# Setup of a two-layer graph kernel reordered, and edge types brought by broadcast transfers

## The chip, the cores and the metric

One core of one Trainium2 chip runs the whole program. The metric is the device time of one execution in microseconds (us); the median of several executions is compared.

## The reference, cut to what is computed

The graph has 1,250 nodes with 512 features and 40,000 edges, sorted by destination. There are 32 relation types, each a mix of 8 bases of 512x512.

```python
h = maximum(layernorm(x), 0)
weight = einsum('rb,bio->rio', w_comp, bases)          # 32 x 512 x 512
h_rel  = einsum('ni,rio->rno', h, weight)
x = x + segment_sum(h_rel[etype, src] * edge_weight, dst) + h_bias
h = maximum(layernorm(x), 0)
g = h @ W.T + b                                        # degree-normalised convolution with self loops
x = x + relu(segment_sum(norm * g[row], col))
```

## The kernel before, in words

**Main loop.** Nodes are cut into 20 destination tiles of 64, and the edges into 335 slots of 128 edges; a slot belongs to one tile. POOL (GpSimd) issues one indirect DMA per slot (L693), which gathers 128 rows of 2,304 bytes from the table `tab0_d` (normalised features as a float16 high and low half, and a one-hot part) into a ring of `UN` = 8 buffers `gath`. PE (TensorE) runs 12 matmuls (L1493, source features against a selection matrix `sel`) and one (L1499, counts for layer 1) for each slot. DVE (VectorE) makes `sel` and `oh_ad` for a batch of up to four slots (`select`, L1125 to L1131), in a ring of three batches, from three columns per slot: `dloc` (place in the tile), `code` (side and block of the source) and `val` (8 numbers, the row of `w_comp` for the edge's type times its weight).

**Steps tied to slots.** `STEPS[s]` lists what each engine does after slot s, in the same order on every engine; `PROD[s]` lists the products with the bases (L1513) that PE weaves into slot s + 1. A `flush` (after slots 12, 24, 37, 48, ...) empties the PSUM banks of a tile, ACT (ScalarE) the high half, DVE the low one. `bsplit` splits one base of 1 MB in two halves, ACT L811 and then DVE L1245; `wt` turns and splits W1 (L1540, L816, L1250). `largest` and `scale` find the powers of two by which bases and W1 are scaled: ACT first takes the sum of squares of each of the 8 bases and of W1 (`squares_of`, L767), and PE waits for all nine at slot 7 before it transposes them (L1360). `turn` (L1522) and `proj` (L1533) are the two steps of layer 1's projection.

**Values.** A value group is eight slots. `types(k)` on PE copies the types of eight slots to all 128 partitions with two matmuls (L1388) of a `band` matrix against `typ16`; DVE compares them with each partition's relation number (`one_hot_types`, L1070) and makes the next `band` (L991); `look(k)` on PE multiplies the one-hot with `wparts` (L1395); DVE reduces and scales (L1079, L1082), ACT takes the high half (L753) and DVE the low half (L1089). Three groups (`VEARLY`) are done in the setup, the others from `STEPS`.

**One shared bank.** The steps types, look, turn, proj, wt, largest and scale all use PSUM bank `MB`. The list `SHARED` is their order, and in `shared_free` PE waits for the reader of the step before: after `types(k)` that is DVE's `one_hot_types(k)`.

**Setup.** SP (SyncE) loads edges and x, writes x to `xbase_d` from SBUF (L567), and loads base 0, then bases 1 to 4 once the edge records are gathered into `padr` (`s_padr`). ACT normalises x tile by tile (L745, L741); the low halves of tiles 0 to 6 are made by POOL (L672), those of tiles 7 to 9 by DVE (`low`, L974) behind most of its setup. SP writes each finished tile to the table (L577), then issues bases 5 to 7, the two bias rows, W1 and the first x rows. DVE turns `padr` into columns (L960 to L969), checks that the edges are in order (the `flag`), makes scales, and then `code` and `dloc` for all 336 columns. A run-time branch on `flag` follows (work for edges in any order; not taken with these inputs). DVE and ACT do the three value groups ahead of it.

Of the kernel before, what the change touches and what calls it, by code (L numbers as in the profile page):

```python
# [6 lines left out]
def gnn_kernel(nc, x, src, dst, etype, ew, bases, w_comp, h_bias, W1, b1, out):  # L7
# [5 lines left out]
    P = 128  # L13
# [20 lines left out]
    TN = 64  # L34
# [49 lines left out]
    VEARLY = 3  # L84
    SLV = NVAL * VB
# [4 lines left out]
    x1_d = nc.dram_tensor("x_layer1", [N, D], f32, kind="Internal").ap()  # L90
    cext_d = nc.dram_tensor("counts_any_order", [2, P, NT * N], f16, kind="Internal").ap()

    ctx = ExitStack()
    with ctx:
# [34 lines left out]
        typ16 = sb("typ16", [P, C0, P], bf16)  # L129
# [9 lines left out]
        rel = sb("rel", [P, 1], f32)  # L139
        ident = sb("ident", [P, P], f32)  # L140
# [47 lines left out]
        w_in = u_t[:, 0:FT, :]  # L188
        TZ = 5
# [7 lines left out]
        blk_c = take_z(i32, P)  # L197
# [15 lines left out]
        e_wt = carve(h_t[:, :])(f32, EC)[0:EP, :]  # L213
# [16 lines left out]
        row_f, same, pack_f = rec_w[0:1, 0:SLP], rec_w[0:1, SLP:3 * SLP], rec_w[0:1, 3 * SLP:3 * SLP + SLP // WPACK]  # L230
# [24 lines left out]
        LOWS, BEARLY = 7, 5  # L255
# [3 lines left out]
        SQ_SETUP, SC_AT, BS_AT, WT_AT = BEARLY, 7, 10, 38  # L259
# [102 lines left out]
        SHARED = []  # L362
        for v in range(VEARLY):
            SHARED += [("types", v), ("look", v)]
        for ss in STEPS:
            SHARED += [k for k in ss if k[0] in ("types", "look", "turn", "proj", "wt", "largest", "scale")]
# [11 lines left out]
        s_win = sem("s_win")  # L378
        s_bias = sem("s_bias")
# [25 lines left out]
        s_scaled = sem("s_scaled")  # L405
# [143 lines left out]
        def _(sp):  # L549
# [20 lines left out]
            for n in range(1, BEARLY):  # L570
                load_base(n)
# [1072 lines left out]
```

## Time and profile before

| | |
|---|---|
| median of 3 runs | 642.95 us (640.42 to 645.22) |
| the profiled execution | 640.33 us, of which the span from first to last instruction is 638.4 us |
| mean granted TensorE clock | 0.912 |
| PE busy | 503.5 us |
| DVE busy | 351.0 us |
| POOL busy | 352.3 us |
| DMA | 129.97 MB, mean 204 GB/s |

The profile is of one execution. Busy time of PE is that of pipelined matmuls, whose ends are modelled. The share of the span tells little by itself, since the setup (to about 65 us), the slots (to about 560 us) and the tail have different limits.

### The profile page before, as it was taken

Reading aid. Unit: us, or ns where it says so; the run is one execution under the profiler, and the core shown is the slowest. Engines: PE = TensorE matmul, PEld = TensorE weight load, DVE = VectorE, ACT = ScalarE, POOL = GpSimd, SP = SyncE. Lnnn points to the kernel's source line nnn. Section 1 sums busy time; section 2 is a strip of 40 time slices with the busy share of each in tenths; the row PEclk is TensorE's granted clock in tenths of the full one; section 3 lists DMA queues with packets and bytes.
Section 4 is the critical chain, followed back from the end, with each engine's and each line's share of the span. In section 5 each row is a group of like instructions: output and inputs, shape, how many; then the busy total and the mean of one; then the engine's idle time right before and its main releaser. Section 6 shows DMA issues by size and latency. Waiting matters only on the chain.

```text
span 638.4 us, 15882 instructions
## 1 busy us (share of the span) xinstructions
PE 503.5 (79%) x5908; PEld 321.6 (50%) x5908; DVE 351.0 (55%) x974; ACT 151.8 (24%) x272; POOL 352.3 (55%) x473
## 2 busy tenths in 40 slices
PE   3031455878978989999999998999987876889997
PEld 1020345545654656665656655565655554545443
DVE  7798178775763445765755655646644321364121
ACT  3492244432220011121220312202201000251021
POOL 3423648765772776675757757767577777400000
PEclk9565767799997999999999999999999978699999
DMA  9888945565783886785866858868768877514042
GB/s 291 300 335 298 346 124 162 143 197 157 219 257 88 231 265 198 211 255 168 265 190 191 264 155 244 255 180 258 230 202 263 237 235 239 160 27 139 2 97 67
DMA packets 44932, 129.97 MB, mean 204 GB/s; under 512 B 9053, under 2 KB 9678, under 8 KB 44854
## 3 DMA queue, kind: packets, MB, share of 16 engines
q0 software_dynamic: 27040, 99.60, 52.5%
q1 hardware_dynamic: 16860, 28.13, 13.5%
q8 instruction: 58, 0.95, 0.6%
q10 hardware_dynamic: 954, 1.13, 0.6%
q14 instruction: 20, 0.16, 0.1%
HBM read 117.83 MB, written 11.00 MB: 202 GB/s over the span
## 4 chain that ended last, share of the span: by engine, by line
PE 50%; DMA 18%; DVE 15%; issue 6%; ACT 5%; POOL 3%; ACTq 1%; SPq 1%; POOLq 0%; DVEq 0%
PE PS L1513 21%; PE PS L1493 16%; DMA gath<-rows_layer,srcs 13%; PE PS L1589 7%; PE PS L1533 5%; DMA u_t<-in_L_gnn_W_dram 4%; DVE zt L1209 2%; POOL gath L693 2%; DVE room_b L1209 2%; ACT room_b L811 2%; DMA edge_records<-room_c 1%; DVE room_b L1245 1%; DMA w1t<-edge_records,w1t 1%; PE PS L1499 1%; ACT zt L800 1%
## 5 line engine op out<-in xcount | busy, mean ns | idle before, releaser
L693 POOL DMA_INDIRECT gath<-rows_layer,srcs x335 | 335.9, 1003 | 179.1 <-PE PS L1499 95.9
L1493 PE MATMUL PS<-sel,gath 128*128 128x48 f16 (+7 forms) x4020 | 299.7, 207 | 58.6 <-DMA gath<-rows_layer,srcs 28.3
L1493 PEld LDWEIGHTS PS<-sel,gath 128*128 128x128 f16 x4020 | 235.2, 103 | 169.4 <-issue 93.5
L1513 PE MATMUL PS<-room_b,zt 128*128 128x512 f16 x480 | 168.3, 392 | 1.6 <-DVE sel L1131 1.5
L1513 PE MATMUL PS<-room_b 128*128 128x512 f16 (+1 forms) x480 | 150.4, 381 | 0.3 <-DVE room_b L1209 0.2
L1499 PE MATMUL PS<-oh_ad,gath 128*128 128x30 bf16 (+7 forms) x335 | 65.0, 194 | 0.0
L753 ACT CAST val<-val_f 128x64 f16<-128x64 f32 x42 | 11.1, 264 | 215.2 <-DVE val_f L1082 215.2
L1125 DVE TENSOR_TENSOR masks<-iota_n,dloc 128x24 bf16<-128x24 f32 (+12 forms) x92 | 17.8, 193 | 78.9 <-issue 40.5
L1513 PEld LDWEIGHTS PS<-room_b 128*128 128x128 f16 (+1 forms) x480 | 47.4, 104 | 14.3 <-issue 1.0
L1513 PEld LDWEIGHTS PS<-room_b,zt 128*128 128x128 f16 x480 | 45.4, 100 | 8.9 <-issue 2.7
L1131 DVE TENSOR_TENSOR sel<-masks,val 128x192 f32<-128x192 bf16 (+12 forms) x92 | 38.6, 419 | 0.0
L1589 PE MATMUL PS<-zt,room_c 128*128 128x512 f16 (+1 forms) x160 | 36.2, 379 | 0.0
L1499 PEld LDWEIGHTS PS<-oh_ad,gath 128*128 128x128 bf16 x335 | 34.4, 103 | 3.1 <-issue 2.6
L1533 PE MATMUL PS<-w1t,hT_t 128*128 128x512 f16 (+1 forms) x120 | 30.1, 405 | 7.4 <-DVE oh_t L1070 5.9
L1079 DVE TENSOR_REDUCE val_f<-PS 128x64 f32<-128x192 f32 x42 | 14.9, 356 | 35.3 <-PE PS L1395 31.3
L1209 DVE SCALAR_TENSOR_TENSOR room_b<-PS,room_b 128x512 f16<-128x512 f32 x40 | 24.8, 682 | 12.9 <-ACT room_b L800 12.9
L1070 DVE TENSOR_SCALAR oh_t<-PS,rel 128x256 bf16<-128x256 f32 x42 | 20.2, 480 | 19.2 <-PE PS L1388 17.5
L800 ACT ACTIVATE room_b<-PS 128x512 f16<-128x512 f32 x40 | 20.6, 601 | 40.1 <-PE PS L1499 37.7
L1127 DVE TENSOR_TENSOR oh_ad<-iota_n,code 128x120 bf16<-128x120 f32 (+12 forms) x92 | 29.6, 322 | 0.0
L1209 DVE SCALAR_TENSOR_TENSOR zt<-PS,zt 128x512 f16<-128x512 f32 x40 | 24.8, 682 | 8.6 <-ACT zt L800 8.6
L803 ACT CAST room_c<-c_i 128x320 f16<-128x320 int32 (+1 forms) x40 | 16.1, 450 | 46.3 <-DVE c_i L1215 46.3
L1589 PEld LDWEIGHTS PS<-zt,room_c 128*128 128x128 f16 (+1 forms) x160 | 16.0, 100 | 18.2
(208 smaller groups left out, 446.0 us busy)
## 6 DMA issues: line engine op xcount, KB each, us to landing
room_b<-in_L_gnn_bases_dram SPq DMA_DIRECT2D x8, 1024.0 KB, 8.2
gath<-rows_layer,srcs POOLq DMA_INDIRECT x335
x_t<-x_base SPq DMA_DIRECT2D x19, 128.0 KB, 5.0
u_t<-in_x_dram SPq DMA_DIRECT2D x9, 256.0 KB, 6.4
x_base<-u_t SPq DMA_DIRECT2D x9, 256.0 KB
x_layer<-x_t SPq DMA_DIRECT2D x18, 128.0 KB
u_t<-x_layer SPq DMA_DIRECT2D x18, 128.0 KB, 2.6
out_dram<-u_t SPq DMA_DIRECT2D x18, 128.0 KB
```

Source lines behind the costliest of these rows:

```text
L693: pool.indirect_dma_start(out=gath[:, s % UN, :], out_offset=None, in_=tab0_d[:, :], in_offset=bass.IndirectOffsetOnAxis(ap=srcs[:, s:s + ...
L800: a.activation(zt[q % 2][:, 0, f, :, TN * h:TN * (h + 1)], zbank(f), ACT.Copy, scale=ZDOWN).then_inc(s_hi, 1)
L1070: v.tensor_scalar(oh_t[:, k % 2, :, :].rearrange("p j e -> p (j e)"), PS[:, MB, 0:VB // 4 * P], rel[:, :], None, ALU.is_equal).then_inc(s_ ...
L1125: v.tensor_tensor(mask, iota_n[:, 0:w].unsqueeze(1).to_broadcast([P, k, w]), dloc[:, s:s + k].unsqueeze(2).to_broadcast([P, k, w]), ALU.is ...
L1127: v.tensor_tensor(oh_ad[:, there, 0:k, 0:HA * w], iota_n[:, 0:HA * w].unsqueeze(1).to_broadcast([P, k, HA * w]), code[:, s:s + k].unsqueez ...
L1131: v.tensor_tensor(sel[:, there, 0:k, 0:NB * w].rearrange("p k (b d) -> p k b d", b=NB), mask.unsqueeze(2).to_broadcast([P, k, NB, w]), val ...
L1209: v.scalar_tensor_tensor(lo, zbank(f), ZDOWN, hi, ALU.mult, ALU.subtract).then_inc(s_lo, 1)
L1493: mm(there, gath[:, s % UN, D * t + P * f:D * t + P * (f + 1)], sel_parts[:, here, k, 0:NB * w, u], start=first and t == 0 and u == 1, sto ...
L1499: mm(there, oh_r[:, s % UN, :], oh_ad[:, here, k, 0:HA * w], start=first, stop=True, skip_group_check=True).then_inc(s_used, 1)
L1513: last = mm(PS[0:r, PBANK[q], :], zt[q % 2][:, t, f, b, 0:r], base_hl[:, b, u, f, :], start=(m == 0), stop=(m == NM - 1))
L1533: last = mm(PS[0:r, MB, :], hT_t[:, s, f, 0:r], w1t[:, t, f, :], start=(f == s == t == 0), stop=(f == FT - 1 and s == 1))
L1589: return mm(PS[0:r, FBANK[j], :], there, u_part(i, t)[0:ROWS[i], :], start=first, stop=True, skip_group_check=not first)
```

## The change

- **W1 first.** W1 is loaded behind x into the unused part of `room_b` (`w_early`), and ACT squares it in the setup. A second load (`s_win2`) brings it to `w_in` for `wt`, which moves from slots 38 to 41 to slots 54 to 57.
- **x_base.** The ten writes from SBUF become one transfer from x in DRAM to `xbase_d`, behind the last base.
- **Loads.** Bases 0 to 3 follow `s_padr`; bases 4 to 7 follow the table and the types of groups 1 and 2. Bias rows wait for all codes.
- **Low halves.** All ten are DVE's, put between its setup steps; POOL makes none.
- **Types.** Two matmuls and `band` per group go. `typ16` is written to DRAM (`types_d`), and for each group SP issues four transfers, each of which copies two slots' types (512 bytes) to 32 partitions, in a ring of three (`TRING`). `one_hot_types` reads SBUF. Steps of kind types leave `SHARED`. Slots within a group are held in another order, which changes access patterns only.
- **Branch and values.** The branch comes ahead of the values. Then one group and 24 columns of codes are done before the first slot; groups 1 to 3 come with slots 0 to 8 and the other 312 columns of codes at slot 4.
- `largest` moves from slot 7 to 9; `bsplit` from slots 10, 13, ..., 31 to 13, 15, 17, 19, 26, 28, 30, 33.

```diff
+        BEARLY = 4
...
+        SQ_SETUP, SC_AT, WT_AT = BEARLY, 9, 54
+        BS_AT = [13, 15, 17, 19, 26, 28, 30, 33]
+        SQ_AT = {4: 0, 5: 1, 6: 3, 7: 6}
+        CFIRST, CODES_AT = VEARLY * VB, 4
...
-        for v in range(VEARLY, NVAL):
-            STEPS[VB * v - 23].append(("types", v))
-            STEPS[VB * v - 18].append(("look", v))
+        for v in range(1, NVAL):
+            at = max(VB * v - 23, 3 * (v - 1))
+            STEPS[at].append(("types", v))
+            STEPS[max(VB * v - 18, at + 2)].append(("look", v))
...
+            sp.dma_start(w_early, W1.rearrange("(c p) i -> p c i", p=P)).then_inc(s_win, 16)
...
+            sp.wait_ge(s_padr, 16 * C0)
+            for n in range(BEARLY):
+                load_base(n)
+            def load_types(v):
+                if v >= TRING:
+                    sp.wait_ge(s_oht, v - TRING + 1)
+                for t in range(FOUR):
+                    s = VB * v + SPG * t
+                    sp.dma_start(types[R * t:R * (t + 1), v % TRING, :],
+                                 types_d[s:s + SPG, :].rearrange("(p j) e -> p (j e)", p=1).to_broadcast([R, SPG * P])).then_inc(
+                                     s_types[v % TRING], 16)
+            sp.wait_ge(s_loc, 2 * C0)
+            for c in range(C0):
+                sp.dma_start(types_d[P * c:P * (c + 1), :], typ16[:, c, :]).then_inc(s_typd, 16)
             for i in range(NT):
-                sp.wait_ge(s_xin[i], 16)
-                sp.dma_start(xbase_d[P * i:P * i + XROWS[i], :], x_in[0:XROWS[i], i, :]).then_inc(s_xbase, 16)
...
+                if i == 4:
+                    sp.wait_ge(s_typd, 16 * C0)
+                    load_types(0)
+                sp.wait_ge(s_h0lo, i + 1)
                 sp.dma_start(tab0_d[P * i:P * i + XROWS[i], 0:2 * D],
                              table_of(i).rearrange("p s d -> p (s d)")).then_inc(s_tab0, 16)
+            for v in range(1, TRING):
+                load_types(v)
             for n in range(BEARLY, NB):
                 load_base(n)
+            sp.dma_start(xbase_d[:, :], x[:, :]).then_inc(s_xbase, 16)
             sp.wait_ge(s_flag, 1)
...
             sp.wait_ge(s_tab0, 16 * (NT + 3))
-            sp.dma_start(w_in, W1.rearrange("(c p) i -> p c i", p=P)).then_inc(s_win, 16)
-            sp.wait_ge(s_xbase, 16 * NT)
+            sp.dma_start(w_in, W1.rearrange("(c p) i -> p c i", p=P)).then_inc(s_win2, 16)
+            load_types(TRING)
+            sp.wait_ge(s_cols, 2)
...
+            sp.wait_ge(s_xbase, 16)
             load_x(0)
             load_x(1)
...
+            for s in range(VEND):
+                for kind, k in STEPS[s]:
+                    if kind == "types" and k + TRING < NVAL:
+                        load_types(k + TRING)
+                    elif kind == "x1" and k < NT - 1:
+                        keep_x1(k)
...
-            for i in range(LOWS):
-                pool.wait_ge(s_h0hi, i + 1)
-                t = table_of(i)
-                g.tensor_tensor(t[:, 1, :], x_in[0:XROWS[i], i, :], t[:, 0, :], ALU.subtract).then_inc(s_h0lo_pool, 1)
...
             def one_hot_types(k):
-                dve.wait_ge(s_types, k + 1)
+                dve.wait_ge(s_types[k % TRING], 16 * FOUR * (k // TRING + 1))
                 if k >= 2:
                     dve.wait_ge(s_look, k - 1)
-                v.tensor_scalar(oh_t[:, k % 2, :, :].rearrange("p j e -> p (j e)"), PS[:, MB, 0:VB // 4 * P], rel[:, :], None,
+                v.tensor_scalar(oh_t[:, k % 2, :, :].rearrange("p j e -> p (j e)"), types[:, k % TRING, :], rel[:, :], None,
                                 ALU.is_equal).then_inc(s_oht, 1)
...
-            def types(k):
-                shared_free(pe, ("types", k))
-                pe.wait_ge(s_band, k + 1)
-                for j in range(VB // 4):
-                    last = mm(PS[:, MB, P * j:P * (j + 1)], band[:, j, :], typ16[:, VB * k // P, :], start=True, stop=True)
-                last.then_inc(s_types, 1)
             def look(k):
                 shared_free(pe, ("look", k))
+                pe.wait_ge(s_oht, k + 1)
...
                     elif kind == "largest":
                         shared_free(pe, ("largest", 0))
-                        pe.wait_ge(s_sqb, NB + 1)
+                        pe.wait_ge(s_sqb, NB)
```

## Rows read from the trace of the kernel before

**Rows 1.** Windows: us, busy us (count) of PE, PEld, DVE, ACT, POOL, granted clock, DMA share, GB/s

```profile
200.00:300.00 100.00, 93.95 (x1218) 61.02 (x1217) 55.43 (x158) 17.30 (x39) 68.34 (x70) 1.00 0.72 213
62.00:64.00 2.00, 0.00 (x0) 0.00 (x0) 2.00 (x9) 1.91 (x3) 1.06 (x1) 0.50 1.04 391
78.00:80.00 2.00, 0.00 (x0) 0.00 (x0) 0.00 (x0) 1.17 (x1) 0.00 (x0) 0.50 1.05 333
```

**Rows 2.** Timeline, PE, setup to slot 25: start, us, instruction, idle before and releaser

```profile
65.74 0.98 PE L1493 MATMUL PS<-sel,gath 128*128 128x80 f16 x12 [7.45 <-DVE sel L1131]
73.91 0.68 PE L1493 MATMUL PS<-sel,gath 128*128 128x80 f16 x12 [0.61 <-DMA gath<-rows_layer,srcs]
80.98 0.37 PE L1360 MATMUL PS<-ident,sq 128*12 128x128 f32 x1 [6.37 <-ACT val L767]
91.98 0.82 PE L1493 MATMUL PS<-sel,gath 128*128 128x88 f16 x6 [5.36 <-DVE zt L1209]
113.86 0.78 PE L1493 MATMUL PS<-sel,gath 128*128 128x80 f16 x6 [6.24 <-DVE zt L1209]
```

**Rows 3.** Timeline, setup, DVE and POOL beside each other

```profile
4.41 0.28 DVE L895 TENSOR_SCALAR ident<-w1t,column 128x128 f32<-128x128 f32 x1
27.71 6.04 POOL L672 TENSOR_TENSOR zt<-u_t,zt 128x512 f16<-128x512 f32 x5 [5.12 <-ACT zt L741]
28.99 1.12 DVE L962 TENSOR_SCALAR w1t<-w1t 128x3 f32<-128x3 f32 x1
32.58 3.76 DVE L967 TENSOR_SCALAR w1t<-w1t 128x128 f32<-128x128 f32 x3
36.25 0.63 DVE L969 CAST typ<-w1t 128x128 bf16<-128x128 f32 x3
49.02 1.87 DVE L974 TENSOR_TENSOR room_c<-u_t,room_c 128x512 f16<-128x512 f32 x3
50.99 0.15 DVE L1043 TENSOR_SCALAR stats<-bound 128x1 int32<-128x1 int32 x1
```

**Rows 4.** Timeline, first and later gathers of POOL

```profile
55.37 1.15 POOL L693 DMA_INDIRECT gath<-rows_layer,srcs  x1 [19.16 <-issue]
65.61 0.95 POOL L693 DMA_INDIRECT gath<-rows_layer,srcs  x1 [0.30 <-issue]
```

**Rows 5.** Timeline, issues of SP

```profile
51.29 1.59 SPq L558 DMA_DIRECT2D room_b<-in_L_gnn_bases_dram  x3
52.92 0.77 SPq L581 DMA_DIRECT2D hb_t<-in_L_gnn_h_bias_dram  x1
55.74 0.39 SPq L607 DMA_DIRECT2D u_t<-in_L_gnn_W_dram  x1
```

**Rows 6.** DMA issues: target, source, queue, count, KB each, us to landing

```profile
hb_t<-in_L_gnn_h_bias_dram SPq DMA_DIRECT2D x1, 256.0 KB, 14.1
u_t<-in_L_gnn_W_dram SPq DMA_DIRECT2D x1, 1024.0 KB, 23.1
zt<-in_L_gnn_w_comp_dram ACTq DMA_DIRECT2D x4, 1.0 KB, 5.1
```

**Rows 7.** Timeline, PE, types of a group and what follows

```profile
300.27 0.27 PE L1388 MATMUL PS<-typ,band 128*128 128x128 bf16 x2
300.38 0.20 PE L1493 MATMUL PS<-sel,gath 128*128 128x72 f16 x1
```

**Rows 8.** Waits of PE, 115 to 200 us: us in total, times, longest

```profile
PE PS L1533 <- DVE oh_t L1070: 4.5, 1, 4.5
```

**Rows 9.** Waits of PE, whole span

```profile
PE PS L1493 <- DMA gath<-rows_layer,srcs: 28.3, 36, 2.2
PE PS L1533 <- DVE oh_t L1070: 5.9, 3, 4.5
```

**Rows 10.** Chain that ended last: start, us, what

```profile
193.00 5.30 PE PS L1533 x12
241.43 2.76 PE PS L1533 x12
```

More of the change, by code:

```diff
@@ L84, in gnn_kernel @@
     VEARLY = 3
+    FOUR = P // R
+    SPG = VB // FOUR
+    TRING = 3
     SLV = NVAL * VB
@@ L361, in gnn_kernel @@
         VEND = max(s for s, ss in enumerate(STEPS) if ss or PROD[s]) + 1
-        SHARED = []
-        for v in range(VEARLY):
-            SHARED += [("types", v), ("look", v)]
+        SHARED = [("look", 0)]
         for ss in STEPS:
-            SHARED += [k for k in ss if k[0] in ("types", "look", "turn", "proj", "wt", "largest", "scale")]
+            SHARED += [k for k in ss if k[0] in ("look", "turn", "proj", "wt", "largest", "scale")]
         SHARED += [("turn", NT - 1), ("proj", NT - 1)]
@@ L493, in shared_free @@
             kind, k = SHARED[n - 1] if n else ("first", 0)
-            if kind == "types":
-                eng.wait_ge(s_oht, k + 1)
-            elif kind == "look":
+            if kind == "look":
                 eng.wait_ge(s_vsum, k + 1)
@@ L1018, in _ @@
-            dve.wait_ge(s_slotmm, 1)
-            begins = PS[0:1, CB, 0:SLP].rearrange("p (g k) -> p g k", k=WPACK)
-            link(v.tensor_copy(pack_f, begins[:, :, WPACK - 1]))
-            for k in reversed(range(WPACK - 1)):
-                there = pack_f if k else slots[0:1, :]
-                link(v.scalar_tensor_tensor(there, pack_f, float(1 << WBITS), begins[:, :, k], ALU.mult, ALU.add))
+            low(0)
+            low(1)
+            columns_max(0)
+            dve.wait_ge(s_slotmm, 1)
@@ L1038, in _ @@
             v.reduce_sum(bad, same[:, 0:NSAME + SL + 1], AX.X).then_inc(s_have, 1)
+            for i in range(8, NT):
+                low(i)
             def powers(lo, hi):
@@ L1447, in _, with look @@
                 pe.wait_ge(s_any_zero, FT + 1)
+            def look(k):
+                shared_free(pe, ("look", k))
+                pe.wait_ge(s_oht, k + 1)
+                for j in range(VB // 4):
+                    last = mm(PS[:, MB, 12 * NB * j:12 * NB * (j + 1)], oh_t[:, k % 2, j, :],
+                              wparts[:, :, :].rearrange("p s c -> p (s c)"), start=True, stop=True)
+                last.then_inc(s_look, 1)
+            pe.wait_ge(s_wparts, 1)
+            look(0)
             window = {}
@@ L1549, in _ @@
                 for kind, k in STEPS[s]:
-                    if kind == "types":
-                        types(k)
-                    elif kind == "look":
+                    if kind == "look":
                         look(k)
```

249 lines of the change are left out of this document (117 added, 132 removed).

## The prediction, made before the changed kernel was run

> **What bounds the kernel now.** Read the windows first: from 200 to 300 us PE is busy 93.95 of 100 us at granted clock 1.00 [rows 1], so once the slots run, what counts is PE's own work and its few waits. The setup is different. In the timeline of PE [rows 2] the first slot starts at 65.74 us; slot 7 starts at 73.91; then PE waits 6.37 us for the squares of W1 and goes on at 80.98; slot 13 starts at 91.98, after 5.36 us of waiting for DVE's flush; slot 25 at 113.86, after 6.24 us for the same. Every microsecond won there by slot 25 stays won unless a gather gives it back, since from there PE is nearly always busy. The DMA windows tell why W1 was late: at 62 to 64 us the engines move 391 GB/s at a share above 1, at 78 to 80 us still 333 [rows 1]. Transfers of one queue land in their order: the bias row issued at 52.92 [rows 5] took 14.1 us [rows 6] and landed at 67.0, W1 issued at 55.74 took 23.1 and landed at 78.8. This order decides most of what follows.
>
> **Part 1: low halves go from POOL to DVE.** While POOL makes low halves (from 27.71 us, seven of them), a DVE instruction on 3 columns takes 1.12 us and three on 128x128 take 3.76 us, 1.25 each; alone, the same kinds take 0.15 us (on one column) and 0.28 us [rows 3]. The stretch L960 to L969, which ends at 36.9 us, holds three such long small instructions (L962, L964 and L965, about 1.1 us each) and the three of 1.25, so it should shrink by about 3 x 0.95 + 3 x 0.97 = 5.7 us. DVE pays ten low halves of 0.62 us (1.87 / 3 [rows 3]), seven more than before, 4.4 us. It gets back 4.8 us, summed from the starts of the instructions between 36.9 and 41.9 us in the same timeline: `band` and its rows 1.0, the packing of windows 1.1, and the check of the order of edges and `wparts` (0.95 and 1.75, moved into waits before `padr`). I let `padr` be ready 1.7 us sooner, as the ten x_base writes no longer stand beside the record writes (0 to 3 us, my estimate). Sum: the last low half ends at 50.9 - 5.7 - 1.7 + 4.4 - 4.8 = 43 us (50.9 is the end of the last low half [rows 3]).
>
> **Part 2: the table.** SP now stands at tile 4 until `typ16` has been written to DRAM. These writes are queued behind bases 0 to 3 (4.2 MB issued at about 26 us; at 0.35 MB per us they end at 38 to 39 us), so I take 40 us for that wait, 42 for the four issues of group 0, and 45.5 for the last table issue. The first gather, at 55.37 before [rows 4], comes at about 49. The first `sel` also moves: flag at 43 us, scales and packing 3 us, the 13 small code instructions of 24 columns about 2.3 us, one value group 1.5 us, one batch 0.9: about 51 us. With the landing of a gather, the first slot starts at about 54 us in place of 65.74, so 11 us sooner (8 to 13).
>
> **Part 3: the queue behind the table.** This is what eats the gain. Behind the last table, SP issues eight type transfers (at about 0.5 us each, 4 us; an issue of a base took 1.59 / 3 = 0.53 [rows 5]), then bases 4 to 7 (4.2 MB), x_base (2.56 MB), W1 again (1.05 MB) and only then the types of group 3. Before, 3.1 MB, two bias rows and W1 stood there. DVE needs group 3 at slot 6, and PE's `look(3)` at slot 8 needs that one-hot: PE can't pass slot 8, and DVE's later work is queued behind the same wait. By then 17 gathers of 0.295 MB (128 x 2,304 bytes) have been issued, 5.0 MB. At 0.37 MB per us, between the 0.391 and 0.333 of [rows 1], the 8.1 + 5.0 = 13.1 MB that begin at about 50 us end at 85 us. So the wait for W1 at slot 7 (80.98 us) is gone, and one for types at slot 8 takes its place. Gathers alone don't bring slot 8 there: under this load one took from 65.61 [rows 4] to 73.91 [rows 2], 8.3 us, and they came some 1.4 us apart, which makes slot 8 possible at 54 + 8 x 1.5 = 66. What ends last without the types would be base 7 and its square: (4.3 + 4.7) / 0.37 = 24.5 us, 74.5, and 2 us on ACT, 76.5. Group 4's types are queued behind the bias rows and the x rows (1.05 MB more, 3 to 4 us), and DVE meets them at step 9 ahead of the scales. From there: one-hot and look 86, slots 9 and 10 88, group 4 at 88.7, scales 2.3 us, 91, and flush(0), now with no `bsplit` ahead of it, lets slot 13 start at 92. **That is 0 against 91.98** [rows 2] (9 us sooner if the types aren't what ends last, 4 later if the copy is slow).
>
> The type transfers after slot 16 I cost at nothing: a group is loaded some 24 slots, over 30 us, ahead, and the nearest rows, four transfers of 1.0 KB in the setup, landed in 5.1 us [rows 6]. If a wait ahead of them on SP (for x1 rows) ate the lead, a group would cost up to 5.1 us, once or twice.
>
> **Part 4: flush(1).** Before, `bsplit` 3 and 4 at slots 19 and 22 stood ahead of the flush at 24, and PE waited 6.24 us [rows 2]. Now four splits end by 19 and the next comes at 26. A flush alone costs PE about 2 us. Gain 4.2 us (2 to 5). The other four splits are as many as fit before slot 37 in both versions: 0 (-1 to +2).
>
> **Part 5: types off PE and out of the shared bank.** In steady running two types matmuls delay the next slot by 300.38 - 300.27 = 0.11 us [rows 7]; groups 5 to 41 make 37 x 0.11 = 4.1 us. The waits are worth more. `proj` waited for `one_hot_types` 4.5 us once, at 188 to 193 us [rows 8], because the step types(12) stood between flush(5) and proj(0); it is now free to run beside the flush. After that idle time the 12 matmuls took 5.30 us, where the next projection took 2.76 [rows 10]: nearly twice, as at a granted clock of 0.50 (1.2 GHz) against 1.00 (2.4 GHz). So this place is worth 4.5 + 2.5 = 7 us. The other waits of this kind are 5.9 - 4.5 = 1.4 [rows 8, 9] and about 2 in smaller lines of the same view (L1522 and L1388), 3.4 together. From 200 us on (3.3 of matmuls, 3.4 of waits) I count half, 3.4, since PE also waits 28.3 us for gathers [rows 9], and time won ahead of a gather that isn't there is lost again. With 0.8 of matmuls ahead of 200 us and the 7: 11.2 us (6 to 15). Moving `wt` to slots 54 to 57 moves its waits of 0.6 to 2 us each to a place with less of DVE's work beside them; of those I count 1.5 us as gone (-1 to 4). DVE's `band` (0.41 us a group) and the cheaper one-hot are off the path: 0.
>
> **Sum.** 0 + 4.2 + 11.2 + 1.5 = 17 us less than 640.33, the profiled execution (638.4 of span and 1.9 around it), so 623. That execution is 2.6 us under the median, 642.95, so the forecast is 626 us, 2.6% less.
>
> **Rivals.** *A: the types of group 3 are not late* (the queue doesn't keep its order, or the copy is quick). Then base 7's squares end last at 76.5: another 9 us, 617. For it: nothing else in the table of steps needs more before slot 9. Against: the two landings of [rows 5, 6], in order of issue. *B, slower: the copy from DRAM to DRAM holds the queue.* No row shows such a copy. At the 391 GB/s of [rows 1] its 2.56 MB take 6.6 us; it decides the sign from the point where it takes 17 us more, 24 us, 0.11 MB per us, so that group 3 lands after 102 us. All that a slower copy adds shows one for one at slot 8, up to 650 if it takes 30 us. A milder form: with 10 of 16 engines it takes 10.5 us, 4 more, 630. No row here shows which; by the rule the forecast would be 630. *C: the gains after slot 25 go back to the gathers.* Then of part 5 only the place at 193 us and a little more stay: 5 to 7 us less, 632. *D: the setup is won, but nothing of it lasts*, because DVE's code columns (13 instructions on 312 columns, some 6 us) and groups 1 to 3, now among slots 0 to 8, become the limit. DVE has them done inside the wait for group 3, so that is no addition to the forecast, but it caps rival A at about 5 us.
>
> **Chances.** Forecast 0.42 (618 to 634), A 0.18 (610 to 618), the milder B 0.12 and C 0.12 (628 to 637), no net change 0.08, B in full 0.08. Range 611 to 640. Differences under 1% (6.4 us) can hardly be told from no change. Faster by over 1%: 0.80; within: 0.12; slower: 0.08.
>
> **What the profile after would show.** L967 near 0.3 us each and no L672; the last table issue at 45 us; the first gather at 49, the first slot at 54; a wait of PE of 15 us or more at `look(3)` released by DVE's one-hot, and DVE idle before it for a DMA of `types`, to 85 us; W1's second load landing just before; slot 13 at 92, slot 25 at 109; no wait of L1533 for the one-hot. I am wrong if the wait at slot 8 ends before 77 or after 95 us, if DVE waits for types after slot 16, or if waits for gathers grow by as much as the types' matmuls and waits shrink.

## The result, and the profile after

The changed kernel takes 633.42 us (median of 14 executions, 629.73 to 638.14); the kernel before, run beside it, 640.75 (14 executions, 636.16 to 645.22). The ratio is 0.9895, 95% interval 0.9864 to 0.9927: faster by 1.1%, some 7 us (less than 2%). The profiled execution took 632.90 us, with a span of 631.0.

The timeline of PE in the changed kernel shows the whole course of the setup: start, duration, instruction, and in brackets the idle time before it with its releaser. L1515 is a slot, L1464 is `look`.

```profile
54.73 0.98 PE L1515 MATMUL PS<-sel,gath 128*128 128x80 f16 x12 [5.76 <-DMA gath<-rows_layer,srcs]
...
69.07 0.32 PE L1464 MATMUL PS<-wparts,oh_t 128*128 128x96 bf16 x2 [4.15 <-DVE oh_t L1097]
...
91.67 0.32 PE L1464 MATMUL PS<-wparts,oh_t 128*128 128x96 bf16 x2 [19.52 <-DVE oh_t L1097]
...
99.22 0.82 PE L1515 MATMUL PS<-sel,gath 128*128 128x88 f16 x6 [3.28 <-DVE zt L1233]
...
115.31 0.32 PE L1464 MATMUL PS<-wparts,oh_t 128*128 128x96 bf16 x2 [6.05 <-DVE oh_t L1097]
...
120.59 0.78 PE L1515 MATMUL PS<-sel,gath 128*128 128x80 f16 x6 [2.93 <-DVE zt L1233]
```

The first slot starts at 54.73 in place of 65.74 [rows 2], 11.0 us sooner. Then `look(3)`, at slot 8, waits 19.52 us for the one-hot of the types, and slot 13 starts at 99.22, 7.2 us *later* than before (91.98). Slot 25 follows at 120.59, 6.7 us later than the 113.86 of before. From slot 25 to the end the kernel before took 638.4 - 113.9 = 524.5 us; this one takes 631.0 - 120.6 = 510.4. So the 7.4 us between the two spans are 14.1 us won behind slot 25, less 6.7 lost ahead of it.

The timeline of DVE names the missing transfer; it also has the low halves (L1022), the step that was L967 in the kernel before (L1015), and the splits of the bases (L1269):

```profile
27.71 0.83 DVE L1015 TENSOR_SCALAR w1t<-w1t 128x128 f32<-128x128 f32 x3
...
40.44 1.27 DVE L1022 TENSOR_TENSOR room_c<-u_t,room_c 128x512 f16<-128x512 f32 x2
```

```profile
91.24 0.29 DVE L1097 TENSOR_SCALAR oh_t<-types,rel 128x256 bf16<-128x256 bf16 x1 [15.13 <-DMA types<-types_by_slot]
...
94.23 0.29 DVE L1097 TENSOR_SCALAR oh_t<-types,rel 128x256 bf16<-128x256 bf16 x1 [0.33 <-DMA types<-types_by_slot]
...
104.46 2.35 DVE L1269 SCALAR_TENSOR_TENSOR room_b<-room_b,scale_i 128x2048 f16<-128x2048 f32 x1 [1.94 <-ACT room_b L841]
...
109.56 2.35 DVE L1269 SCALAR_TENSOR_TENSOR room_b<-room_b,scale_i 128x2048 f16<-128x2048 f32 x1 [0.47 <-ACT room_b L841]
...
112.61 2.35 DVE L1269 SCALAR_TENSOR_TENSOR room_b<-room_b,scale_i 128x2048 f16<-128x2048 f32 x1
...
115.07 2.35 DVE L1269 SCALAR_TENSOR_TENSOR room_b<-room_b,scale_i 128x2048 f16<-128x2048 f32 x1
```

DVE stood still for 15.13 us up to 91.24, released by a DMA into `types`. SP's issues (start, time that the issues took, count) and two landings (count, KB, us from issue to landing) say why it came so late:

```profile
45.14 6.86 SPq L586 DMA_DIRECT2D types<-types_by_slot  x8
52.05 2.66 SPq L569 DMA_DIRECT2D room_b<-in_L_gnn_bases_dram  x4
54.75 6.75 SPq L604 DMA_DIRECT2D x_base<-in_x_dram  x1
63.16 0.39 SPq L629 DMA_DIRECT2D u_t<-in_L_gnn_W_dram  x1
63.62 8.26 SPq L586 DMA_DIRECT2D types<-types_by_slot  x4
...
84.61 2.43 SPq L626 DMA_DIRECT2D x_t<-x_base  x4
87.08 9.16 SPq L586 DMA_DIRECT2D types<-types_by_slot  x16
```

```profile
x_base<-in_x_dram SPq DMA_DIRECT2D x1, 2500.0 KB, 29.8
...
u_t<-in_L_gnn_W_dram SPq DMA_DIRECT2D x1, 1024.0 KB, 27.1
```

x_base landed at 54.75 + 29.8 = 84.6, W1 at 63.16 + 27.1 = 90.3, and the four transfers of group 3 behind them at 91.2. A landing is the last of 16 increments of a semaphore, and the trace has the time of each. For x_base fourteen came from 82.2 to 82.7 and two at 84.5 and 84.6; for W1 fourteen from 85.8 to 88.0, the others at 89.0 and 90.2; of the 64 of group 3 the first came at 86.0, before W1 had landed, and the last eight from 89.3 to 91.2. So the queue keeps its order only roughly, and each landing waits for the last few increments. An issue isn't free either: x_base occupied SP for 6.75 us, the eight types behind the table for 6.86, four more for 8.26. The windows (us of PE, PEld, DVE, ACT, POOL, then clock, DMA share, GB/s) show the queue, between 80 and 88 us with all five of these at rest:

```profile
76.00:80.00 4.00, 0.00 (x0) 0.00 (x0) 0.11 (x1) 2.00 (x2) 0.00 (x0) 0.50 1.21 502
80.00:84.00 4.00, 0.00 (x0) 0.00 (x0) 0.00 (x0) 0.00 (x0) 0.00 (x0) 0.50 0.78 242
84.00:88.00 4.00, 0.00 (x0) 0.00 (x0) 0.00 (x0) 0.00 (x0) 0.00 (x0) 0.50 1.02 351
88.00:92.00 4.00, 0.33 (x4) 0.25 (x5) 0.76 (x4) 0.00 (x0) 0.00 (x0) 0.50 0.80 187
99.22:120.59 21.37, 11.83 (x160) 10.18 (x161) 17.88 (x31) 10.56 (x12) 15.83 (x11) 0.66 0.51 143
```

From 76 to 80 us the DMA engines move 502 GB/s, from 80 to 84 only 242, and from 88 to 92 only 187. In steps of 1 us the two low places differ: from 80 to 82 the DMA share is 0.43 and 0.52, though W1 and two bias rows are queued; from 88 to 90 it is 1.05 and 0.95, at 252 and 204 GB/s, while the small transfers of types land. The last of the lines covers slots 13 to 24 and is read further down.

PE's waits for gathers in slots and products, from the waits of PE over the whole span (us, times, longest):

```profile
PE PS L1515 <- DMA gath<-rows_layer,srcs: 32.5, 38, 5.8
...
PE PS L1535 <- DMA gath<-rows_layer,srcs: 4.0, 4, 1.5
```

Waits of `proj` for the one-hot, 5.9 us before [rows 9], are gone. Those for gathers went from 28.3 to 32.5 in the slots, which includes the 5.76 before the first slot, and 4.0 more stand in the products (L1535), which had none before. The place that the prediction priced at 7 us, the first `proj` (L1555), now has no wait, and its 12 matmuls take 2.75 us where they took 5.30 [rows 10]:

```profile
193.09 2.75 PE L1555 MATMUL PS<-w1t,hT_t 128*128 128x512 f16 x12
```

### The profile page after: what moved, and what is told of

Read it like the earlier page. It is cut to its first block, busy times and chain, and to the rows that moved or that the text cites. A ratio compares the mean times of both kernels' runs of the same rounds, so it can differ in the third digit from the quotient of the medians.

```text
span 631.0 us, 15843 instructions
## 1 busy us (share of the span) xinstructions
PE 495.5 (79%) x5824; PEld 317.0 (50%) x5824; DVE 327.6 (52%) x948; ACT 152.2 (24%) x273; POOL 340.6 (54%) x466
## 4 chain that ended last, share of the span: by engine, by line
PE 52%; DMA 18%; DVE 12%; issue 6%; POOL 4%; ACT 3%; SPq 3%; POOLq 0%; DVEq 0%; ACTq 0%
PE PS L1535 22%; PE PS L1515 17%; DMA gath<-rows_layer,srcs 12%; PE PS L1612 7%; PE PS L1555 4%; POOL gath L722 4%; DMA types<-types_by_slot 3%; DMA room_b<-in_L_gnn_bases_dram 2%; SPq L586 2%; DVE room_b L1233 1%; DMA types_by_slot<-h_t 1%; DVE zt L1233 1%; DVE stats L955 1%; PE PS L1521 1%; ACT room_b L830 1%
## 5 line engine op out<-in xcount | busy, mean ns | idle before, releaser
L722 POOL DMA_INDIRECT gath<-rows_layer,srcs x335 | 332.4, 992 | 188.1 <-issue 95.6
L1515 PE MATMUL PS<-sel,gath 128*128 128x48 f16 (+7 forms) x4020 | 299.1, 207 | 52.8 <-DMA gath<-rows_layer,srcs 32.5
L1515 PEld LDWEIGHTS PS<-sel,gath 128*128 128x128 f16 x4020 | 234.8, 103 | 164.4 <-issue 86.0
L1535 PE MATMUL PS<-room_b,zt 128*128 128x512 f16 x480 | 167.7, 391 | 1.9 <-DMA gath<-rows_layer,srcs 1.9
L1535 PE MATMUL PS<-room_b 128*128 128x512 f16 (+1 forms) x480 | 150.0, 380 | 2.7 <-DMA gath<-rows_layer,srcs 2.1
L1535 PEld LDWEIGHTS PS<-room_b 128*128 128x128 f16 (+1 forms) x480 | 47.2, 104 | 16.4 <-DMA gath<-rows_layer,srcs 2.4
L1535 PEld LDWEIGHTS PS<-room_b,zt 128*128 128x128 f16 x480 | 45.1, 100 | 8.9 <-DMA gath<-rows_layer,srcs 2.1
L1464 PE MATMUL PS<-wparts,oh_t 128*128 128x96 bf16 x84 | 11.0, 215 | 37.8 <-DVE oh_t L1097 36.3
L1555 PE MATMUL PS<-w1t,hT_t 128*128 128x512 f16 (+1 forms) x120 | 28.3, 386 | 1.4 <-DVE val_f L1104 1.4
L830 ACT ACTIVATE zt<-PS 128x512 f16<-128x512 f32 x40 | 20.6, 600 | 20.2 <-PE PS L1521 20.2
## 6 DMA issues: line engine op xcount, KB each, us to landing
x_base<-in_x_dram SPq DMA_DIRECT2D x1, 2500.0 KB, 29.8
```

The costliest lines, as they stand in the source:

```text
L722: pool.indirect_dma_start(out=gath[:, s % UN, :], out_offset=None, in_=tab0_d[:, :], in_offset=bass.IndirectOffsetOnAxis(ap=srcs[:, s:s + ...
L830: a.activation(zt[q % 2][:, 0, f, :, TN * h:TN * (h + 1)], zbank(f), ACT.Copy, scale=ZDOWN).then_inc(s_hi, 1)
L1515: mm(there, gath[:, s % UN, D * t + P * f:D * t + P * (f + 1)], sel_parts[:, here, k, 0:NB * w, u], start=first and t == 0 and u == 1, sto ...
L1535: last = mm(PS[0:r, PBANK[q], :], zt[q % 2][:, t, f, b, 0:r], base_hl[:, b, u, f, :], start=(m == 0), stop=(m == NM - 1))
L1555: last = mm(PS[0:r, MB, :], hT_t[:, s, f, 0:r], w1t[:, t, f, :], start=(f == s == t == 0), stop=(f == FT - 1 and s == 1))
```

## The experiments

My theory was that the order of SP's one queue sets the time ahead of slot 13, that DVE's work sets the time from there to slot 25, and that everything later is the freed bank. Ratios are to the kernel before, run on the same chip; in brackets the 95% interval. The times of slots are of one profiled execution each. Kernels e9, e10 and e11 ran on a chip where the kernel before took 750.57 us; of these only ratios, and times up to slot 25, are set against the others.

**e1: types of groups 3 and 4 ahead of the big transfers**

```diff
-            for v in range(1, TRING):
+            for v in range(1, TRING + 1):
                 load_types(v)
             for n in range(BEARLY, NB):
                 load_base(n)
+                if n == BEARLY + 1:
+                    load_types(TRING + 1)
...
-            load_types(TRING)
...
-                    if kind == "types" and k + TRING < NVAL:
+                    if kind == "types" and TRING + 1 < k + TRING < NVAL:
```

`TRING` stays 3, so these are groups 3 and 4.

> The changed kernel with the types of groups 3 and 4 queued ahead of the big loads: group 3 before base 4, group 4 between bases 5 and 6. Theory (the queue keeps its order, and x_base and W1 in front of group 3 hold slot 8): the 19.5 us wait of PE at look(3) and the 15.1 us wait of DVE before it go; what ends last is then base 7 and its squares, landed at 77.6 us in the changed kernel, so slot 13 starts at about 88 to 90 us in place of 99.2 and the kernel is 9 to 11 us faster than the changed one, about 623. Rival (the bases are what holds the slots, since ACT takes their squares ahead of the values of groups 1 to 3): look(3) then waits for ACT and the bases instead, slot 13 comes at 95 or later, gain under 4 us.

621.66 us, 0.9758 [0.972, 0.9797], span 619.5. PE's timeline:

```profile
74.02 0.32 PE L1465 MATMUL PS<-wparts,oh_t 128*128 128x96 bf16 x2 [7.75 <-DVE oh_t L1098]
...
81.18 0.32 PE L1465 MATMUL PS<-wparts,oh_t 128*128 128x96 bf16 x2 [4.08 <-DVE oh_t L1098]
...
89.09 0.82 PE L1516 MATMUL PS<-sel,gath 128*128 128x88 f16 x6 [2.80 <-DVE zt L1234]
...
110.46 0.78 PE L1516 MATMUL PS<-sel,gath 128*128 128x80 f16 x6 [2.94 <-DVE zt L1234]
```

The long wait is gone; slots 13 and 25 come 10.1 us sooner than in the changed kernel, and slot 25 to the end takes 509.0. Eight transfers of 16 KB moved in one queue are worth some 11 us (e3, below, ran on the same chip and took 632.46). What is left is a wait at `look(2)`, since ACT's half of group 1 stands behind its squares of base 5.

**e2: group 3 alone**: e1's edit without `load_types(TRING + 1)` and without its last change, so that group 4 still comes behind the x rows

> Only the types of group 3 are queued ahead of base 4; group 4 stays behind x_base, W1, the bias rows and the x rows. Theory: PE passes slot 8, but DVE then stands at group 4's one-hot, which it meets before the scales, until group 4 lands (94.2 us in the changed kernel), so flush(0) and slot 13 don't come sooner: 0 to 2 us gained, about 632. Rival (only the look at slot 8 holds PE): the gain is the same as with both groups early, 9 us.

637.5 us, 0.9984 [0.9958, 1.001], span 638.9 (the profiled execution was the slowest of ten). That is no gain over the kernel before, and I had expected one of 0 to 2 us over the changed kernel. PE, and SP's issues of group 4 and those behind it:

```profile
79.60 0.32 PE L1463 MATMUL PS<-wparts,oh_t 128*128 128x96 bf16 x2 [4.07 <-DVE oh_t L1096]
...
103.25 0.82 PE L1514 MATMUL PS<-sel,gath 128*128 128x88 f16 x6 [18.53 <-DVE zt L1232]
```

```profile
87.20 13.53 SPq L586 DMA_DIRECT2D types<-types_by_slot  x16
```

`look(3)` starts at 79.60, and then PE waits 18.53 us for flush(0): DVE meets group 4 ahead of the scales and the flush. The wait moved by one group, and to slot 13 it became 4 us longer. That group stood behind x_base, W1 and the x rows, and DVE's one-hot of it came at 98.73 us, not at the 94.2 that I had taken from the changed kernel. A single late group is enough.

**e5: x_base written from SBUF, as in the kernel before**, so that no copy stands in front of W1 and group 3

```diff
+            for i in range(NT):
+                sp.wait_ge(s_xin[i], 16)
+                sp.dma_start(xbase_d[P * i:P * i + XROWS[i], :], x_in[0:XROWS[i], i, :]).then_inc(s_xbase, 16)
...
-            sp.dma_start(xbase_d[:, :], x[:, :]).then_inc(s_xbase, 16)
...
+            act.wait_ge(s_xbase, 16 * NT)
```

> The changed kernel with x_base written as before: ten transfers from SBUF in the early setup, none from DRAM to DRAM behind the bases. Theory (the copy stood ahead of group 3: issued at 54.8 us, landed at 84.6, 7 us after base 7): group 3 lands at 83 to 84 us in place of 91.2, slot 13 starts at about 92, 6 to 8 us faster than the changed kernel, about 626. The early setup may lose 1 to 2 us of that, since ACT waits for the ten writes. Rival (what counts is only the share of the gathers in the queue, not the copy): less than 2 us.

628.17 us, 0.9797 [0.9755, 0.9839], span 628.8.

```profile
87.08 0.32 PE L1468 MATMUL PS<-wparts,oh_t 128*128 128x96 bf16 x2 [12.23 <-DVE oh_t L1101]
...
94.94 0.82 PE L1519 MATMUL PS<-sel,gath 128*128 128x88 f16 x6 [3.56 <-DVE zt L1237]
```

Slot 13 is 4.3 us sooner than in the changed kernel, though the first slot (58.00) is 3.3 later: the ten writes come back into the early setup, and ACT waits for them. I had expected slot 13 at 92. Taking the copy out of the queue is thus worth the 4.3 us and what the later setup took back.

**e11: the copy cut into 1,248 rows and 2 rows**

```diff
-            sp.dma_start(xbase_d[:, :], x[:, :]).then_inc(s_xbase, 16)
+            cut = N // 16 * 16
+            sp.dma_start(xbase_d[0:cut, :], x[0:cut, :]).then_inc(s_xbase, 16)
+            sp.dma_start(xbase_d[cut:N, :], x[cut:N, :]).then_inc(s_xbase, 16)
```

> The changed kernel with the copy to x_base cut in 1,248 rows (16 x 78) and 2 rows. Theory A (a copy of 1,250 rows uses 10 of the 16 engines): the copy, which landed at 84.6 us, 7.0 behind base 7, lands 3 to 4 us sooner, group 3 at 87 to 88, 3 to 4 us faster than the changed kernel, 629.5. Theory B (the rows are merged or spread over all engines anyway): landing and time unchanged within 1 us.

742.59 us, 0.9865 [0.9806, 0.9923] (on the slow chip). The copy was issued at 54.57 and took 28.4 us in place of 29.8; slot 13 starts at 100.19 and slot 25 at 121.56, against 99.22 and 120.59, and up to slot 25 the waits of `look` for the one-hot are 32.0 us (36.3 in the changed kernel).

Nothing is won by a number of rows that 16 divides. The Trainium skill, "DMA: Bandwidth & Descriptors", Why a DMA increments its semaphore by 16 and not by 1, would have given the copy of 1,250 rows 10 engines. The traces show no sign of it: the copy of 1,250 rows landed at 84.6 us and the two parts of the cut one at 84.2, and the 16 increments of its semaphore came from 82.2 to 84.6, spread like those of a load of 1 MB (base 7: 75.0 to 77.5). Whether the rows are merged before the rule applies is not shown.

**e10 and e12: the types of groups 1 to 4 issued by ACT**, on its own queue; e12 is the same kernel on a chip of the usual speed

```diff
+            act.wait_ge(s_typd, 16 * C0)
+            act_types(1)
+            act_types(2)
...
             val_hi(0)
+            act_types(3)
+            act_types(4)
...
-            for v in range(1, TRING):
-                load_types(v)
             for n in range(BEARLY, NB):
...
-            load_types(TRING)
...
-                    if kind == "types" and k + TRING < NVAL:
+                    if kind == "types" and TRING + 1 < k + TRING < NVAL:
```

> The types of groups 1 to 4 are issued by ACT on its own queue (1 and 2 behind wtT, 3 and 4 behind the first high half of values); SP issues bases 4 to 7 right behind the table. Theory (the order of one queue is what held the types, and SP's 8.9 us of type issues in e1 held the bases): no wait for types, although x_base and W1 are queued at the same time as before; bases are issued at 45 instead of 54 us and base 7 lands 7 us sooner than in e1, slot 13 at 82 to 84 us in place of 89.1, 614 to 616. Rival 1 (the engines are busy whatever the queue, so small transfers wait on any queue): a wait for types of 5 us or more stays. Rival 2 (gathers and DVE are the limit by now): 620 to 622, as e1.

> The same kernel as the run with the types issued on ScalarE's queue, on a chip that may be of the ordinary kind (kernel before near 641 us). My theory (the order of SP's one queue made group 3's types late, and nothing after slot 25 depends on it): the first slot near 59.5 us, slot 13 near 85 and slot 25 near 107, as in that run, since the set-up's times did not differ between the chips, and then 509 to 512 us to the end as in the changed kernel, so a span of 616 to 619 us and a ratio to the kernel before of 0.966 to 0.974. Rival (the saving was bound to the other chip, where everything after slot 25 was slow): ratio 0.976 or above, as with groups 3 and 4 issued early.

e10: 732.0 us, 0.9723 [0.9659, 0.9787]. e12: 617.93 us, 0.963 [0.9593, 0.9667], span 614.1, the fastest of all: 23 us below the kernel before, and by the ratios 17 below the changed one (the spans, 614.1 and 631.0, say the same). PE, and ACT's issues:

```profile
58.66 0.98 PE L1527 MATMUL PS<-sel,gath 128*128 128x80 f16 x12 [9.92 <-DMA gath<-rows_layer,srcs]
...
83.60 0.79 PE L1527 MATMUL PS<-sel,gath 128*128 128x88 f16 x6 [2.72 <-DVE zt L1245]
...
104.93 0.78 PE L1527 MATMUL PS<-sel,gath 128*128 128x80 f16 x6 [2.93 <-DVE zt L1245]
```

```profile
44.81 2.50 ACTq L804 DMA_DIRECT2D types<-types_by_slot  x3
...
47.34 3.41 ACTq L804 DMA_DIRECT2D types<-types_by_slot  x5
...
51.76 4.83 ACTq L804 DMA_DIRECT2D types<-types_by_slot  x8
```

Slot 13 starts at 83.60, 15.6 us sooner than in the changed kernel. The same kind of transfer is on time, although bases and x_base are queued on SP from 45.90 us on: the bytes of the types were never what made them late, only their place behind others in one queue. (Groups 3 and 4 were issued from 51.76 us, and their last increments came at 60.3 and 63.1.) SP now issues the bases 6 us sooner, beside the first gather, and the first slot, released by that gather, starts at 58.66 in place of 54.73: that the one is the price of the other is likely, not tested. e10 (slot 13 at 85.23, slot 25 at 106.61) came near what I expected of it, and e12 was slightly faster than I expected. From slot 25 to the end it takes 509.2 us, like e1.

**e6: e1 with the squares of bases 5 to 7 and the scales moved later**, so that ACT does not hold up group 1

```diff
-        SQ_SETUP, SC_AT, WT_AT = BEARLY, 9, 54
-        BS_AT = [13, 15, 17, 19, 26, 28, 30, 33]
-        SQ_AT = {4: 0, 5: 1, 6: 3, 7: 6}
+        SQ_SETUP, SC_AT, WT_AT = BEARLY, 13, 54
+        BS_AT = [15, 17, 19, 21, 26, 28, 30, 33]
+        SQ_AT = {4: 6, 5: 9, 6: 11, 7: 12}
```

> e1 with the squares of bases 4 to 7 at slots 6, 9, 11, 12 in place of 0, 1, 3, 6, the largest at 13 and four splits at 15, 17, 19, 21. Theory (in e1 PE waits 7.7 and 4.1 us at look(2) and look(3), because ACT stands at the squares of a base not yet landed, ahead of the high half of a value group): both waits shrink to 1 us, flush(0) comes some 10 us sooner, and the wait moves to the scales, which need base 7 (landed at about 80 us); slot 25 at 104 to 106 us in place of 110.5 and 4 to 6 us faster than e1, 617. Rival (gathers are the limit there): the waits for gathers grow by the same amount and the time stays at 621 to 622.

625.47 us, 0.9737 [0.9673, 0.98] (on another chip than e1): no different from e1. PE, and the one line of DVE with its wait:

```profile
81.56 0.82 PE L1516 MATMUL PS<-sel,gath 128*128 128x88 f16 x6 [6.24 <-DVE zt L1234]
...
86.91 0.37 PE L1391 MATMUL PS<-ident,sq 128*12 128x128 f32 x1 [3.12 <-ACT val L792]
...
104.33 0.32 PE L1465 MATMUL PS<-wparts,oh_t 128*128 128x96 bf16 x2 [6.06 <-DVE oh_t L1098]
...
111.86 0.78 PE L1516 MATMUL PS<-sel,gath 128*128 128x80 f16 x6 [5.17 <-DVE zt L1234]
```

```profile
103.89 0.29 DVE L1098 TENSOR_SCALAR oh_t<-types,rel 128x256 bf16<-128x256 bf16 x1 [4.33 <-DMA types<-types_by_slot]
```

Slot 13 starts 7.5 us sooner than in e1, and slot 25 is 1.4 later. The 7.5 us went into a wait for the last square (3.12), into one at `look(5)` (6.06), for which DVE waited 4.33 us for group 5's types (they too stand behind the x rows in SP's queue), and into flush(1) (5.17, 2.2 more than e1's). My expectation fell: I had freed one wait of several that end within a few microseconds of each other.

**e3: the splits spread as before**, at slots 13, 16, 19, 22 in place of 13, 15, 17, 19

> bsplit 1 to 3 at slots 16, 19, 22 in place of 15, 17, 19. Theory (between two flushes it is DVE's sum of work that counts, not where the splits stand): the 6.0 us wait at look(5) goes, but the wait of flush(1) grows from 2.9 to about 8 us, slot 25 stays at 120.6 us, time the same within 1 us. Rival (packing three splits ahead of types(5) costs by itself): slot 25 comes 5 to 6 us sooner and the kernel is 5 us faster, 628.

632.46 us, 0.9919 [0.9889, 0.9949], span 630.4.

```profile
113.02 0.32 PE L1464 MATMUL PS<-wparts,oh_t 128*128 128x96 bf16 x2 [3.77 <-DVE oh_t L1097]
...
120.55 0.78 PE L1515 MATMUL PS<-sel,gath 128*128 128x80 f16 x6 [5.17 <-DVE zt L1233]
```

The wait at `look(5)` is shorter (3.77 for 6.05) and that for flush(1) longer (5.17 for 2.93); slot 25 starts at 120.55 against 120.59. Where these splits stand between the two flushes doesn't matter.

**e4: types back in the order of the shared bank**, from step 25 on, with no matmuls

```diff
-        for ss in STEPS:
-            SHARED += [k for k in ss if k[0] in ("look", "turn", "proj", "wt", "largest", "scale")]
+        for at, ss in enumerate(STEPS):
+            SHARED += [k for k in ss if k[0] in ("look", "turn", "proj", "wt", "largest", "scale") or (k[0] == "types" and at >= 25)]
...
+            if kind == "types":
+                eng.wait_ge(s_oht, k + 1)
```

> The changed kernel with the old waits of the shared bank put back from slot 25 on: the step types(k) issues no matmul, but the next user of the bank waits for the one-hot of group k, as before. Theory: the wait of proj(0) for the one-hot behind flush(5) comes back, 4.5 us and with it projection matmuls at half the clock (5.3 in place of 2.7 us), and 2 to 3 us of small ones; 7 to 9 us slower than the changed kernel, about 641. Rival (the gain after slot 25 is that of the removed matmuls and of DVE's freed time): at most 2 us slower.

642.95 us, 1.0083 [1.0052, 1.0114], span 639.3; slot 25 at 120.27, and 519.0 us from there to the end, 8.6 more than in the changed kernel. Waits for the one-hot, L1557 being `proj` and L1546 `turn`:

```profile
PE PS L1557 <- DVE oh_t L1099: 5.5, 3, 4.4
...
PE PS L1546 <- DVE oh_t L1099: 1.4, 2, 1.0
```

```profile
197.83 5.08 PE L1557 MATMUL PS<-w1t,hT_t 128*128 128x512 f16 x12 [4.39 <-DVE oh_t L1099]
```

The two lines of [rows 8, 9] are back with nearly their old sizes (5.5 and 4.4 for 5.9 and 4.5), and the 12 matmuls behind the longest wait take 5.08 us again in place of 2.75. e3, which ran beside it, was 10.5 us faster.

**e8: e4 with two matmuls per group as well** (on constants, in the place of the types' own)

> e4 (the old bank waits from slot 25 on) with two matmuls of 128 columns added at each step of kind types, on constants, written to the same bank and read by nobody. Theory (a pair costs PE 0.11 us and a wait for the bank now and then): 36 groups make 4 us and 1 to 2 us of waits, so from slot 25 to the end 523 to 525 us, as in the kernel before (524.5), in place of 519.0 in e4; about 4 us slower than e4, 647. Rival (the matmuls fall into waits for gathers): at most 1 us over e4.

643.52 us, 1.004 [1.0007, 1.0073]; slot 25 at 118.62, 521.1 us to the end, 2.1 more than e4, and less than the 4 or so that I expected. The medians don't part the two kernels: 643.52 against 642.95, with the ratios the other way round (1.004 and 1.0083). So the rival, at most 1 us, holds as well as a cost of 2 us.

**e9: `wt` back at slots 38 to 41**

> The changed kernel with the four wt steps back at slots 38 to 41. Theory (what is left of the 14.1 us won from slot 25 to the end, after 8.6 for the bank waits and about 2 for the matmuls, is the place of wt, beside less of DVE's work): 3 us slower than the changed kernel, 636.5, from slot 25 to the end 513 to 514 us in place of 510.4. Rival (the place doesn't matter, DVE's freed band and one-hot time is the rest): within 1 us of the changed kernel.

747.53 us, 0.995 [0.9912, 0.9988] (slow chip); 624.1 us from slot 25 to the end, against 619.9 in e11, which ran beside it with `wt` at 54. The place of `wt` is worth about 4 us on this chip: all ten executions of e9 (744.59 to 751.35) lie above all four of e11 (740.69 to 743.30), which differs from it in the cut copy as well. The intervals of the two ratios just overlap (0.9912 and 0.9923), so the size is rough.

**e7: the kernel before with all low halves on DVE**, nothing else changed

```diff
-        LOWS, BEARLY = 7, 5
+        LOWS, BEARLY = 0, 5
```

> The kernel before with all ten low halves on DVE behind the flag, none on POOL. Theory (POOL's low halves make DVE's small instructions long): L962, L964 and L965 take 0.2 us in place of 1.0 to 1.2 and the three of L967 0.3 each in place of 1.25, so the first low half starts 5 to 6 us sooner than 49.0, and the last ends 1 to 2 us sooner or at the same time than 50.9, as seven more come at 0.62 us each; the time of the kernel is that of before within 2 us, since W1 still ends its wait. Rival (these instructions are long by themselves, or by DMA traffic): no change of their durations, and the last low half ends 4 us later.

639.58 us, 0.9994 [0.9968, 1.0021], span 635.8. DVE beside a resting POOL, and PE at slot 7:

```profile
28.51 0.17 DVE L962 TENSOR_SCALAR w1t<-w1t 128x3 f32<-128x3 f32 x1
...
29.31 0.82 DVE L967 TENSOR_SCALAR w1t<-w1t 128x128 f32<-128x128 f32 x3
```

```profile
79.91 0.37 PE L1360 MATMUL PS<-ident,sq 128*12 128x128 f32 x1 [7.90 <-ACT val L767]
```

The instruction on 3 columns took 1.12 us beside POOL's low halves and takes 0.17 without; the three on 128x128 went from 3.76 to 0.82 [rows 3]. Not every instruction was slowed: L961 and L963 took 0.15 and 0.16 us in the kernel before too, while POOL was busy. The last low half ends 2.0 us sooner (48.9 for 50.9), yet the time is the same, since PE then waits longer for the squares of W1 (7.90 for 6.37 us): a setup that ends sooner is worth nothing in front of a late transfer.

## Why the prediction was right or wrong

I forecast 626 us against a median of 642.95, so 2.6% less; measured are 1.1%. The kind and the places were right, the size was not: of 17 us of gain, 7.4 showed in the spans.

**Part 1, right.** L1015's three took 0.83 us, the small instructions 0.15 to 0.17, `padr` was there by 26.1 us (SP, which waits for it, issued the bases at 26.08), some 2 us sooner than before, and the last low half ended at 41.7 (forecast 43). e7 shows the cause, POOL's low halves, by itself.

**Part 2, right.** Last table issue 45.1 (45.5), first gather 50.87 (49), first slot 54.73 (54).

**Part 3, right mechanism, wrong size; this is the larger error.** I wrote that the wait for W1 would go and one for group 3's types would take its place at slot 8, behind W1's second load. That is what PE's and DVE's timelines show, and e1, e2 and e12 confirm it by moving the transfers alone. The failed term is "13.1 MB that begin at about 50 us end at 85 us" at 0.37 MB per us. In its place the trace has a begin at 52.05 and an end at 91.2. The issues behind the table took 6.9 us and not 4, which is 2 us of the 6.2. The bytes that I counted were about right (bases, copy and W1 8 MB, 17 gathers issued by 73.42), but they took 39.2 us, so 0.33 MB per us and not 0.37. Three things stand in those windows that a rate of the full queue leaves out. The first window, from 52 to 56 us, has only 275 GB/s. The ten windows of 4 us from 52 to 92 sum to 14.1 MB: the bias rows and the first x rows, 1 MB that I had queued behind group 3, moved in part beside it. And the landings wait for the last increments: the last two of x_base came 1.8 us behind the other fourteen, those of W1 1.0 and 2.2, and the last eight of group 3's 64 took from 89.3 to 91.2. How the rest of the 6.2 us splits among these three is not shown. Slot 13 then came 8.0 us behind the types, where I had 7. Together 7.2 us: 92 became 99.22.

**Part 4, wrong: 0.5 us in place of 4.2.** I counted which splits stand "ahead of the flush at 24" in the list of steps. In time, the same four stand between flush(0) and flush(1) in both kernels: before at 97.22, 102.31, 106.10 and 109.15 us, after at 104.46, 109.56, 112.61 and 115.07, each 2.35 us of DVE. The windows from slot 13 to slot 25 say it in one line; for the kernel before it is this one, to be set against the last line of the windows above:

```profile
91.98:113.86 21.88, 12.60 (x162) 10.90 (x163) 18.45 (x32) 10.57 (x12) 16.04 (x11) 0.66 0.50 141
```

DVE is busy 18.45 of 21.88 us before and 17.88 of 21.37 after, and the rest is mostly short waits for ACT's half of its work: 0.57 us less work, 0.51 us less time. e3 moves the splits and changes neither (17.88 of 21.31); e1 (17.89 of 21.37) and e12 (17.90 of 21.33) have the same sum and length with other setups. That DVE's sum sets the length is the reading of these windows; no run takes more work off DVE there. The failed step is thus the count of splits ahead of the flush, and the 2 us for a flush alone: four splits were there as before. My 6.24 us of waiting were real, but what they waited for was DVE's sum; fewer splits "ahead" only turned part of that wait into one at `look(5)`.

**Part 5, right: 14.1 us against 12.7** (11.2 and 1.5 for `wt`). The place at 193 us gave both its wait and the half-speed matmuls back, and e4 takes both away again. e4 puts 8.6 us of the 14.1 on the bank's order (by the medians of e3 and e4 10.5), e8 0 to 2 on the matmuls, e9 about 4 on the place of `wt`. The figures from slot 25 on are from single profiled executions, and the times of one kernel spread over 8 us (629.73 to 638.14), so the smaller two are rough. That `wt` is worth more than the 1.5 I gave it, and the matmuls rather less than the share of 4.1 that I counted, is likely; the sum holds. Transfers of types behind slot 25 cost DVE nothing: of its 42 one-hots only two waited for a DMA, at 91.24 and 94.23 us.

**Rivals.** The time, 633.42 us, lies at the upper end of the forecast's range and inside those of the milder B and of C as well, so it doesn't choose among them; the traces do. A (types not late) is what e12 makes: 617.93 us, near its 617, but by a queue of its own. That D would cap A at about 5 us did not hold: groups 1 to 3 and 312 code columns fitted beside the slots, and e12 gained some 17. B in full is refused by the copy's landing 7.0 us behind base 7 (77.6 to 84.6), and its mild form by that too, since I had taken 10.5 us for ten engines and 6.6 for all; the increments and e11 say the same. C is refused by the 14.1 us that stayed. PE's waits for gathers from slot 25 on, slots and products together, are 27.1 us where they were 26.0: the gathers took back about 1 us.

**Left open.** Why an issue on SP takes 0.4 us at one time and 6.75 at another isn't explained: megabytes were queued on SP in both cases. Nor is it why the DMA share falls to 0.43 from 80 to 81 us with W1 queued. Why the matmuls of e8 cost as little as they seem to isn't settled either, and the chip of e9 to e11, slow behind slot 25 only, wasn't looked into.

## What to carry to other kernels

A wait that is removed uncovers the next transfer in the same queue: list what is issued between it and the next thing that someone needs, and move small, urgent transfers ahead or to another engine's queue (here worth 10 to 16 us ahead of slot 13, for 128 KB in e1 and 256 KB in e12). Reckon the end of a queue with the time of its issues, with what is queued behind, and with the last increments of each landing, not with the rate of a full queue alone (0.33 MB per us here, not 0.37). Where one engine is busy more than eight tenths of a stretch between two fixed points, sum its work there before giving a gain to any new order of it.

## What the hardware showed that I had not expected

- One DMA issue on SP took from 0.39 us (W1 at 63.16) to 6.75 us (x_base at 54.75), and four issues of 16 KB 8.26 us (the first of them 6.67), all of these, the short one too, with megabytes still queued there. Sixteen such issues took 10.7 us on ACT in e12.
- With the copy from DRAM to DRAM in the queue, the window from 76 to 80 us had 502 GB/s and a DMA share of 1.21, against 361 to 425 with loads and gathers, and the next one, with the copy not yet landed, 242 and 0.78.
- The last two of a transfer's 16 increments came 1 to 2 us behind the other fourteen (x_base and W1 in the changed kernel), and in the kernel before W1's came 3.5 us behind (75.1, then 78.6 and 78.8).
- A POOL tensor operation beside DVE made DVE's instruction on 3 columns 6.6 times as long (1.12 for 0.17 us, e7 against [rows 3]), but left two others on 3 columns as they were.
- The same kernel took 750.57 us on one chip and 638 to 641 on others; there slot 25 of e11 came as early as elsewhere (121.56), and all of the difference lay behind it.
